# Attention and mixture-of-experts layer: accumulating two PSUM banks side by side, and moving the bias term of the router

## What is computed

```python
Q, K, V = X @ W_q + b_q, X @ W_k + b_k, X @ W_v + b_v
A = softmax(Q @ K.T / sqrt(1024))            # one head of 1024
x = layernorm(X + A @ V)
scores = softmax(x @ gate_w.T)               # 8 experts
idx = top_k(scores + gate_b, 2)              # rw: the scores of those two, else 0
h_e = silu((x @ w1[e] + b1[e]) * (x @ w3[e] + b3[e]))      # 1408 wide
y = sum over e of rw[:, e] * (h_e @ w2[e] + b2[e])
z = the same expert function with the shared weights sw1, sw3, sw2
out = layernorm(x + y + z)
```

## Time and profile before

| | us |
|---|---|
| median of 5 runs | 8086.62 |
| the five runs | 7471.01, 7544.67, 8086.62, 8194.12, 8262.0 |
| the profiled execution, its own time | 7450.74 |
| its span on the slowest core (core 1) | 7449.0 |
| TensorE busy with matmuls | 5698.7 (77%) |
| VectorE busy | 2995.0 (40%) |
| ScalarE busy | 748.3 (10%) |
| spans of the 8 cores | 7429.6 to 7449.0 |

### The profile page before, as it was taken

The page is one execution under the profiler, slowest core; times in us unless marked ns, Lnnn a source line. Parts: engine busy times, 40 slices in busy tenths (PEclk is TensorE's granted clock), DMA queues, the critical chain, the costliest instruction groups (busy, mean ns, idle before and its releaser), DMA issues.

```text
span 7449.0 us, 73824 instructions; the slowest of 8 cores (7429.6 to 7449.0 us)
## 1 busy us (share of the span) xinstructions
PE 5698.7 (77%) x26324; PEld 2566.5 (34%) x26324; DVE 2995.0 (40%) x5512; ACT 748.3 (10%) x1121; POOL 128.4 (2%) x156
## 2 busy tenths in 40 slices
PE   6986666666660699999079999908999970999996
PEld 2432222222220244444034444403444430444443
DVE  2344444444441433333443333344333334433334
ACT  0001010010010011111001111101111110111111
POOL 0000000000000000000000000000000000000000
PEclk9997778788875799999589999958999995999998
DMA  3111001010016053543405435341453542235431
GB/s 64 40 32 34 26 26 34 26 34 26 26 30 116 1 94 56 85 77 64 103 6 88 74 67 94 54 96 27 67 94 55 86 80 70 47 54 87 75 66 39
DMA packets 233109, 431.77 MB, mean 58 GB/s; under 512 B 72327, under 2 KB 80648, under 8 KB 232750
## 3 DMA queue, kind: packets, MB, share of 16 engines
q0 software_dynamic: 138128, 334.52, 27.7%
q1 hardware_dynamic: 94622, 92.54, 4.1%
HBM read 694.44 MB, written 50.33 MB: 100 GB/s over the span
## 4 chain that ended last, share of the span: by engine, by line
PE 74%; DVE 11%; DMA 9%; issue 4%; ACT 1%; DVEq 1%; SPq 0%; ACTq 0%; POOL 0%; POOLq 0%
PE p3h L862 18%; PE p3o L898 18%; PE p3h L870 18%; PE p2o L641 7%; PE p2s L589 7%; DMA x2fm<-x2b_scr 3%; DMA out<-y_sb 2%; DVE st L613 2%; PE p1f L489 2%; DMA qblk<-q_scr 2%; PE p1f L506 1%; DMA q_scr<-qstage 1%; DVE at_sb L631 1%; DVE gtmp L786 1%; PE p2a L627 1%
## 5 line engine op out<-in xcount | busy, mean ns | idle before, releaser
L862 PE MATMUL p3h<-x2fm,w 128*128 128x512 bf16 x6336 | 1503.6, 380 | 0.0
L870 PE MATMUL p3h<-x2fm,w 128*128 128x512 bf16 x6336 | 1500.3, 380 | 0.0
L898 PE MATMUL p3o<-w_sb,h_sb 128*128 128x512 bf16 x6336 | 1373.3, 379 | 71.2 <-ACT h_sb L886 71.2
L876 DVE TENSOR_SCALAR t1r<-p3h,b1c 128x512 f32<-128x512 f32 x792 | 594.5, 751 | 784.6 <-PE p3h L862 754.9
L882 DVE SCALAR_TENSOR_TENSOR t1r<-p3h,b3c,t1r 128x512 f32<-128x512 f32 x792 | 594.3, 750 | 773.1 <-PE p3h L870 773.1
L898 PEld LDWEIGHTS p3o<-w_sb,h_sb 128*128 128x128 bf16 x6336 | 617.4, 98 | 827.1 <-issue 87.9
L862 PEld LDWEIGHTS p3h<-x2fm,w 128*128 128x128 bf16 x6336 | 621.0, 98 | 752.2 <-issue 8.4
L870 PEld LDWEIGHTS p3h<-x2fm,w 128*128 128x128 bf16 x6336 | 621.1, 98 | 751.5 <-issue 6.8
L886 ACT ACTIVATE h_sb<-t1r 128x512 bf16<-128x512 f32 x792 | 499.3, 630 | 3503.5 <-DVE t1r L882 3503.5
L589 PE MATMUL p2s<-k_sb,qblk 128*128 128x512 bf16 x2048 | 500.2, 410 | 381.1 <-DMA qblk<-q_scr 381.1
L905 DVE SCALAR_TENSOR_TENSOR y_sb<-p3o,rw_all,y_sb 128x512 f32<-128x512 f32 x512 | 384.2, 750 | 899.2 <-PE p3o L898 899.2
(11 more groups left out here) (100 smaller groups left out, 2042.1 us busy)
## 6 DMA issues: line engine op xcount, KB each, us to landing
w<-w1s POOLq DMA_DIRECT2D x36, 2816.0 KB, 39.2
w<-w3s POOLq DMA_DIRECT2D x36, 2816.0 KB, 53.2
w_sb<-w2s POOLq DMA_DIRECT2D x36, 2816.0 KB, 22.4
xres<-x SPq DMA_DIRECT2D x32, 512.0 KB, 6.5
x_scr<-x2stage SPq DMA_DIRECT2D x32, 512.0 KB, 3.3
y_sb<-x_scr SPq DMA_DIRECT2D x4, 4096.0 KB, 14.7
out<-y_sb SPq DMA_DIRECT2D x32, 512.0 KB, 7.2
xblk<-x POOLq DMA_DIRECT2D x8, 1024.0 KB, 8.2
```

The lines of the kernel that those rows point to most:

```text
L862: E_.matmul(o, l, r, start=st, stop=sp),
L870: E_.matmul(o, l, r, start=st, stop=sp),
L876: E_.tensor_scalar(o, i, bb, None, OP.add),
L898: E_.matmul(o, l, r, start=st, stop=sp),
```

## The change

Four edits, all in the order of the code.

(a) In the scores, chunks are taken in pairs: the matmuls of two banks alternate, and VectorE's four instructions follow behind the pair. (b) In the product with V and in the experts' second stage, the two halves of the output alternate in `p2o0`/`p2o1` and `p3o0`/`p3o1`, so that two matmuls in a row have the same left operand; the two VectorE instructions follow behind both. (c) The routing matmuls go to `p3o0` and `p3o1` in turn, and the bank `p3g` is gone. (d) The bias part is moved from ahead of the experts to behind the first stage of expert 0.

```diff
     def p2_s_stats(qb):
-        for sc in range(nsc):
-            bank = sc % 4
+        for scg in range(0, nsc, 2):
+            scs = [sc for sc in (scg, scg + 1) if sc < nsc]
             for dc in range(nkc):
...
+                for sc in scs:
+                    bank = sc % 4
+                    prog.op("tensor",
...
+            for sc in scs:
+                bank = sc % 4
+                prog.op("vector",
...
-        for (v0, vl) in splits(DK, 512):
-            ob = v0 // 512
-            for tc in range(ntc):
+        vparts = splits(DK, 512)
+        for tc in range(ntc):
+            for (v0, vl) in vparts:
+                ob = v0 // 512
                 prog.op("tensor",
...
+        for (v0, vl) in vparts:
+            ob = v0 // 512
             prog.op("vector",
...
-    gps = ps("p3g", [128, 512], F32, p3ps)
...
         for j in range(nj):
+            gb_ = ops_[j % 2]
+            b_gb_ = b_ops[j % 2]
             for dc in range(ndc):
                 prog.op("tensor",
-                        lambda E_, o=gps[:, 0:E],
+                        lambda E_, o=gb_[:, 0:E],
...
+            if e == 0:
+                for j in range(nj):
+                    prog.op("vector",
+                            lambda E_, o=rwp[:, 0:E], i=rw_all[:, j * E:(j + 1) * E]:
+                            E_.tensor_copy(o, i),
...
             for j in range(nj):
-                for (v0, vl) in splits(D, 512):
-                    ob = (j * ((D + 511) // 512) + v0 // 512) % 2
-                    for hc in range(nhc):
+                dparts = splits(D, 512)
+                for hc in range(nhc):
+                    for (v0, vl) in dparts:
+                        ob = v0 // 512
                         prog.op("tensor",
...
+                for (v0, vl) in dparts:
+                    ob = v0 // 512
                     if e < E:
                         prog.op("vector",
```

More of the change, by code:

```diff
@@ L580, in p2_s_stats @@
         par = qb % 2
-        for sc in range(nsc):
-            bank = sc % 4
+        for scg in range(0, nsc, 2):
+            scs = [sc for sc in (scg, scg + 1) if sc < nsc]
             for dc in range(nkc):
[L584 to L598, removed]
+                for sc in scs:
+                    bank = sc % 4
+                    prog.op("tensor",
+                            lambda E_, o=sbank[bank][:],
+                            l=qblk[slot][:, dc * 128:(dc + 1) * 128],
+                            r=k_sb[:, dc * S + sc * 512: dc * S + sc * 512 + 512],
+                            st=(dc == 0), sp=(dc == nkc - 1):
+                            E_.matmul(o, l, r, start=st, stop=sp),
+                            reads=[b_qblk[slot], b_ksb], writes=[b_sbank[bank]])
+            for sc in scs:
+                bank = sc % 4
+                prog.op("vector",
+                        lambda E_, o=stats[par][:, sc:sc + 1], i=sbank[bank][:]:
+                        E_.reduce_max(o, i, AX, negate=True),
+                        reads=[b_sbank[bank]], writes=[b_stats[par]])
+                prog.op("vector",
+                        lambda E_, o=s_sb[par][:, sc * 512:(sc + 1) * 512],
+                        i=sbank[bank][:]: E_.tensor_copy(o, i),
+                        reads=[b_sbank[bank]], writes=[b_ssb[par]])
         prog.op("vector",
@@ L708, in build_core_program @@
     b_ops = [Buf(f"p3o{i}") for i in range(2)]
-    gps = ps("p3g", [128, 512], F32, p3ps)
-    b_gps = Buf("p3g")
     rtp = ps("p3r", [128, 1024], BF16, p3ps)
@@ L759, in build_core_program @@
                         E_.matmul(o, l, r, start=st, stop=sp),
-                        reads=[b_x2fm[xslot], b_gwt], writes=[b_gps])
-            prog.op("vector", lambda E_: E_.tensor_copy(lg[:], gps[:, 0:E]),
-                    reads=[b_gps], writes=[b_lg])
+                        reads=[b_x2fm[xslot], b_gwt], writes=[b_gb_])
+            prog.op("vector", lambda E_, i=gb_[:, 0:E], br=b_gb_:
+                    E_.tensor_copy(lg[:], i),
+                    reads=[b_gb_], writes=[b_lg])
             prog.op("vector",
@@ L887, in build_core_program @@
                             reads=[b_t1r[tsl]], writes=[b_hsb])
+            if e == 0:
+                for j in range(nj):
+                    prog.op("vector",
+                            lambda E_, o=rwp[:, 0:E], i=rw_all[:, j * E:(j + 1) * E]:
+                            E_.tensor_copy(o, i),
+                            reads=[b_rw], writes=[b_rwp])
+                    prog.op("tensor",
+                            lambda E_, o=rtp[0:EE, j * 128:(j + 1) * 128], i=rwp[:, 0:EE]:
+                            E_.transpose(o, i, idb[:]),
+                            reads=[b_rwp, b_rwp_one, b_idb], writes=[b_rtp])
+                prog.op("vector",
+                        lambda E_: E_.tensor_copy(rwt[0:EE, 0:TT], rtp[0:EE, 0:TT]),
+                        reads=[b_rtp], writes=[b_rwt])
+                for j in range(nj):
+                    for (v0, vl) in splits(D, 512):
+                        ob = (j * ((D + 511) // 512) + v0 // 512) % 2
+                        prog.op("tensor",
+                                lambda E_, o=ops_[ob][:, 0:vl],
+                                l=rwt[0:EE, j * 128:(j + 1) * 128],
+                                r=b2all[0:EE, v0:v0 + vl]:
+                                E_.matmul(o, l, r, start=True, stop=True),
+                                reads=[b_rwt, b_b2all], writes=[b_ops[ob]])
+                        prog.op("vector",
+                                lambda E_, o=y_sb[:, j * D + v0: j * D + v0 + vl],
+                                i=ops_[ob][:, 0:vl]:
+                                E_.tensor_tensor(o, o, i, OP.add),
+                                reads=[b_ops[ob], b_ysb], writes=[b_ysb])
             for j in range(nj):
-                for (v0, vl) in splits(D, 512):
-                    ob = (j * ((D + 511) // 512) + v0 // 512) % 2
-                    for hc in range(nhc):
+                dparts = splits(D, 512)
+                for hc in range(nhc):
+                    for (v0, vl) in dparts:
+                        ob = v0 // 512
                         prog.op("tensor",
```

## The result

| | before | changed |
|---|---|---|
| median of all runs, us | 7974.85 (10 runs) | 8187.89 (6 runs) |
| lowest run, us | 7453.64 | 7930.15 |
| comparable runs, ratio | 1 | 1.0608, interval 1.0517 to 1.0698 |

The change makes the kernel 6.1% slower.

What follows compares the result with a forecast made beforehand. TensorE was taken to bound the expert stages, a chain through several engines attention. 415 + 2 + 31 + 20 - 13 = 455 us on 7450.74 gave 7906 us; own range 7800 to 8040, the range given up to 8560.

Steps and rivals of the forecast that it cites:

- Hand-over of the banks: Experts' second stage: both banks finish together, so each hand-over costs 1.66 us (ninth expert 1.53) in two waits, +415 us.
- The waits of attention: Attention: TensorE waits longer for the copy behind the scores, +31 us, and for the `qblk` load, +20 us.
- I put no clock cost on their growth: Attention: TensorE's clock has fallen before it restarts anyway, so the longer waits add no time at low clock.
- Bias part: Expert 0: moved part gains 24.8 us at the start, loses 21.5 us between the stages, -13 us for four tiles.
- The fallen clock in the second stage: Rival, experts' second stage: short breaks drop TensorE to 1.2 GHz, +1270 us, together 9170 us; chance 5%.
- The shared operand: Rival, matmuls sharing a left operand: each saves up to 0.098 us, -511 us, so 7395 us; chance 4%.
- The half-paid hand-over: Rival, experts' second stage: the wait for bank 1 vanishes, costing 260 in place of 415 us, 7751 us; chance 8%.
- A bias part wholly hidden: Rival, expert 0: the moved bias part costs nothing between the stages, 7820 us; chance 3%.

Runs made afterwards that it cites:

- the run with four banks: Kernel before with the alternating second stage alone, blocks taking p3o0/p3o1 and p3h2/p3h3 in turn; die medians 7431 and 7434 us, against 7438 us before.

## Why the prediction was right or wrong

**The figure of 7906 us: wrong as a time of this kernel's median.** The sum was right and its base was not. The text took 7450.74 of the profiled execution, added 455, and named 8542 as the same sum on the median. Beside the shown median of 8086.62, 7906 reads as 2% faster, in a text that says 6% slower. The changed kernel's median over all runs is 8187.89, between the two figures and under the 8560 to which the range reached. The step that failed is "I forecast for runs like the profiled one": the five times shown lay in two clusters, three of them in the upper one, and the median of a handful of runs may fall in either. What can be forecast is the ratio, and the median shown should carry it. By ratio the forecast was (7450.7 + 455) / 7450.7 = 1.061, and 1.0608 was measured. That agreement is closer than the terms deserve: against the span of 494 us the sum of 455 is 39 us short: 37 are missing in attention, and 12 too few in the second stage and 10 too few of gain in the bias part nearly cancel.

**Hand-over of the banks: right, in mechanism and size.** Predicted 6.41 us per block, measured 6.40; two waits of 0.86 and 0.48 us idle, clock 1.00; with four banks nothing of it is left. For the edit alone +417 was forecast, and +412 and +429 were measured by span, +422 in the tiles.

**The waits of attention: right. Their clock: wrong.** TensorE's wait for the copy was forecast at 7.2 us and is 7.16; the longer wait for the load, 0.64 us more, is 0.68. The step that failed is "I put no clock cost on their growth". It was reasoned that the clock has fallen anyway before TensorE starts. It has, but how long it then stays low changed: the rise came 5.2 us after the start of the scores in place of 3.4, and attention cost +88 us in place of 51. The bounds, 30 to 100 us, held it; they allowed for a low clock that lasts longer behind each longer wait, which is what happened.

**Bias part: right in sign, mis-sized.** 23 us of span gained where 13 were forecast, 17 of them in the tiles. The parts can be read from core 1 of the run with these edits alone, as means of four tiles, against core 1 of the kernel before. The last matmul of expert 0's first stage comes 25.0 us sooner after the first routing matmul (forecast 24.8; in the changed kernel the 33rd matmul starts 100.8 us after it, forecast 100.9). From there to the second stage it is 17.8 us longer (forecast 18.6), and the second stage is 1.9 us longer (forecast 2.9, the restart at the low clock). The net gain is 5.2 us per tile in place of 3.3: the step that was mis-sized is the loss, 21.5 us forecast and 19.7 measured.

**The rivals.** The fallen clock in the second stage: excluded by the trace (1.00 over eight changed second stages). The breaks of 0.9 and 0.5 us behind each block don't lower it. By the Trainium skill ("TensorE: Matmul & The Clock Gate", section "A second HAM failure mode: psum-queue depth-cycling") frequent small idle breaks between groups of matmuls that cycle through PSUM banks let the clock swing. This trace, with 1.00, doesn't show it. The shared operand: excluded by the run with four banks. The half-paid hand-over: excluded, both waits are there. A bias part wholly hidden: excluded by the 23 us.

## What to carry to other kernels

Count the time that a PSUM bank has to be drained before it is wanted again: when two accumulations are interleaved, both banks end together, and two buffers become one. Swapping the loops cost nothing here once there was a second pair of banks, but with matmuls that already follow each other every 0.216 us, the columns' own pace, it gained nothing either. Where executions fall into clusters, forecast a ratio. And split a difference of spans by stage before adding parts up: a stage that an edit doesn't touch can differ by several us.

## What the runs showed of the hardware

In attention, TensorE stops twice in each query block and restarts at 1.2 GHz. The moment at which it was granted 2.4 GHz didn't keep a fixed distance from its start: 3.4 us in the kernel before, 5.2 with both attention edits, 4.4 when it waited 1.1 us longer still. That last wait cost 7 to 23 us over 31 blocks in place of 35, and the period of a block stayed at 58 us, while the two edits, whose waits add 1.6 us per block, had moved it from 55.1 to 57.8. So a small delay ahead of a restart can cost nearly twice itself (the edit in the product with V: 22 us of waiting, 42 us of span) or a fraction of itself. Whether a small saving there may likewise give less than itself was not tried. A single delay was tried, so how the cost goes between these points is open.
